# A graph network kernel: more groups of gathered rows fetched outside GpSimd's queue, from lists of byte offsets

## What is computed

```python
def reference(x, src, dst, edge_attr_32, ...):
    h = relu(layernorm(x))
    neigh1 = segment_sum(h[src], dst) * inv_deg          # round 0
    neigh2 = segment_sum(neigh1[src], dst) * inv_deg     # round 1
    x = x + 0.5 * neigh1 + 0.5 * neigh2
    h = relu(layernorm(x))
    for W_msg, W_edge, W_root, b in layers:              # rounds 2 and 3
        msg = h[src] @ W_msg + edge_attr_32 @ W_edge
        agg = segment_max(msg, dst)                      # 0 where a node has no edge
        h = leaky_relu(agg + h @ W_root + b)
    return x + h
```

## Time and profile before

| | |
|---|---|
| Time, median of 3 runs | 12477.9 us (12459.53 to 12489.42) |
| Span of the profiled execution, first to last instruction | 8075.9 us |
| The profiled execution's time around the span | not given on the page |
| POOL busy | 5983.3 us (74%), 6410 instructions |
| PE busy | 5063.4 us (63%) |
| DVE busy | 3315.1 us (41%) |
| ACT busy | 1517.2 us (19%) |
| Granted PE clock, mean share of full speed | 0.678 |
| DMAs of one row: SP, ACT, tail | 10240, 5120, 256 |
| Indirect DMAs of POOL | 6128 |

### The profile page before, as it was taken

The page is one execution under the profiler, slowest core; times in us unless marked ns, Lnnn a source line. Parts: engine busy times, 40 slices in busy tenths (PEclk is TensorE's granted clock), DMA queues, the critical chain, the costliest instruction groups (busy, mean ns, idle before and its releaser), DMA issues.

```text
span 8075.9 us, 156597 instructions
## 1 busy us (share of the span) xinstructions
PE 5063.4 (63%) x26211; PEld 3792.9 (47%) x26211; DVE 3315.1 (41%) x7073; ACT 1517.2 (19%) x5246; POOL 5983.3 (74%) x6410
## 2 busy tenths in 40 slices
PE   3444444445444444444677888787787788878878
PEld 2333333334333333333555655565575565556556
DVE  5444444445433333333533433333343343333335
ACT  2000000001000000000322333333342333333334
POOL 6777777776777777777677777777767777777776
PEclk7555555556555555555677888888797787888888
DMA  3111111111211111111144434444433443444443
GB/s 92 42 42 41 42 41 42 41 41 46 57 42 42 41 42 41 41 41 41 41 94 93 98 89 96 93 98 93 92 72 92 97 98 87 97 93 97 93 92 79
DMA packets 337350, 553.38 MB, mean 69 GB/s; under 512 B 212648, under 2 KB 212648, under 8 KB 311848
## 3 DMA queue, kind: packets, MB, share of 16 engines
q0 software_dynamic: 196096, 301.60, 18.2%
q1 hardware_dynamic: 129796, 243.57, 11.9%
q10 hardware_dynamic: 10788, 2.16, 0.2%
HBM read 521.97 MB, written 24.87 MB: 68 GB/s over the span
## 4 chain that ended last, share of the span: by engine, by line
POOL 53%; issue 21%; PE 11%; SPq 9%; DMA 3%; DVE 2%; ACT 1%; DVEq 0%; ACTq 0%; POOLq 0%
POOL rows L449 53%; SPq L296 5%; SPq L319 3%; PE ps L702 3%; PE ps L700 3%; DMA rows<-table,src_sb 2%; PE ps L724 2%; PE ps L807 1%; SPq L302 1%; PE ps L713 1%; DMA arena<-in_eat 1%; PE ps L681 0%; PE ps L818 0%; ACT arena L493 0%; DMA table<-arena 0%
## 5 line engine op out<-in xcount | busy, mean ns | idle before, releaser
L449 POOL DMA_INDIRECT rows<-table,src_sb x6128 | 5790.9, 945 | 1958.6 <-issue 1849.1
L681 PE MATMUL ps<-arena,rows 128*98 128x128 f32 (+1 forms) x6088 | 1513.6, 429 | 2097.1 <-DMA rows<-table,src_sb 1446.2
L681 PEld LDWEIGHTS ps<-arena,rows 128*98 128x98 f32 (+1 forms) x6088 | 1259.8, 276 | 2373.4 <-DVE comp L927 1990.2
L942 DVE TENSOR_TENSOR_SCAN arena<-arena,ps 96x512 f32<-96x512 f32 x782 | 997.6, 1276 | 2433.9 <-PE ps L702 2409.3
L927 DVE TENSOR_TENSOR comp<-comp,ps 98x128 f32 (+1 forms) x3128 | 894.7, 286 | 2158.4 <-PE ps L681 1841.9
L700 PE MATMUL ps<-arena,we 32*96 32x512 f32 x1564 | 993.7, 719 | 765.1 <-DMA rows<-table,src_sb 415.9
L702 PEld LDWEIGHTS ps<-ident,rows 128*96 128x96 f32 x6168 | 823.5, 187 | 714.4 <-issue 714.4
L910 DVE TENSOR_TENSOR arena<-ps,meta 128x512 f32<-128x512 f32 x1564 | 1050.7, 672 | 29.2 <-issue 25.7
L518 ACT COPY comp<-ps 96x128 f32 x3128 | 818.8, 262 | 1057.6 <-PE ps L724 796.4
L702 PE MATMUL ps<-ident,rows 128*96 128x128 f32 x6168 | 1013.5, 316 | 0.0
L724 PE MATMUL ps<-arena 128*96 128x128 f32 x6256 | 932.8, 299 | 0.9 <-ACT arena L509 0.9
(11 more groups left out here) (104 smaller groups left out, 1404.2 us busy)
## 6 DMA issues: line engine op xcount, KB each, us to landing
side<-table SPq DMA_DIRECT2D x10240, 0.4 KB
arena<-flags SPq DMA_DIRECT2D x194, 768.0 KB
rows<-table,src_sb POOLq DMA_INDIRECT x6128
side<-table ACTq DMA_DIRECT2D x5120, 0.4 KB
arena<-in_eat SPq DMA_DIRECT2D x194, 256.0 KB
table<-arena SPq DMA_DIRECT2D x56, 336.0 KB, 2.8
out<-xs SPq DMA_DIRECT2D x13, 336.0 KB
tail<-table SPq DMA_DIRECT2D x256, 0.4 KB
```

The source lines that it names most:

```text
L449: pool.indirect_dma_start(rows[:, g % RING, j, 0:D], None, tables[r][:, :], bass.IndirectOffsetOnAxis(src_sb[:, c:c + 1], 0)).then_inc(lan ...
L681: m = pe.matmul(ps[0:w, at + k * P:at + (k + 1) * P], got[k][:, 0:w], hot[:, j % HOTS, k, :], start=True, stop=True)
L942: dve.tensor_tensor_scan(run[:, slot % SCANS], fe[0:D, slot // UNIT, q * W:(q + 1) * W], ps[0:D, ROWS + slot % 2 * BANK:ROWS + slot % 2 * ...
```

## The change

`PLAN[r][e]` is now (first, step, n): n groups from `first` on, `step` apart; a group that would fall on place 0 or 1 of its sweep moves to place 2. In the sums these are groups 50, 94, 140, 186, 234, 278, 324, 370 on SP and 44, 90, 138, 182, 228, 274, 322, 366 on ACT, 16 in a round. In the maxima SP takes 60, 122, 186, 246, 308, 370, and ACT, which took none, 92, 182, 274, 362: 10 in a round.

A new input `order` holds `src` in edge order, one row of 512 numbers for each group. SP loads the rows of the groups aside, and that of the last group, into partitions of the new tile `low` (whose partition 0 is `base`), and DVE multiplies them by 384 once, so they are byte offsets (three more steps in `prep`). `side_rows` and `tail_rows` load 32 neighbouring numbers at once and use each as the offset of a DMA of 384 bytes, with no product between. SP and ACT in the sums, and SP in the maxima, issue a group as 16 such blocks; in the maxima SP spreads the blocks over the feature loads ahead of the group, and PE waits on one semaphore for each of the four batches.

In the maxima ACT's sweeps are unrolled, and each step of `extract` ends with `fetch_pair`: on even groups a load of 12 offsets and six DMAs, on odd groups the other six, 43 pairs for a group aside.

```diff
-PLAN = {r: {0: (9, 2), 1: (9, 3)} for r in (0, 1)} | {r: {0: (9, 0)} for r in (2, 3)}
+BLOCK = 32
+PAIR = 12
+PLAN = {r: {0: (48, 46, 8), 1: (44, 46, 8)} for r in (0, 1)} | {r: {0: (60, 62, 6), 1: (92, 90, 4)} for r in (2, 3)}
...
-SIDES = {r: {e: (SWEEPS - 1) // span for e, (span, _) in PLAN[r].items()} for r in PLAN}
-ASIDE = {r: {(b + 1) * PLAN[r][e][0] * RING + PLAN[r][e][1]: (e, b) for e in PLAN[r] for b in range(SIDES[r][e])} for r in PLAN}
+SIDES = {r: {e: [g + max(0, 2 - g % RING) for g in range(first, first + step * n, step)] for e, (first, step, n) in PLAN[r].items()} for r in PLAN}
+ASIDE = {r: {g: (e, b) for e in SIDES[r] for b, g in enumerate(SIDES[r][e])} for r in PLAN}
+LISTS = {(0, 0): 32, (1, 0): 32, (0, 1): 64, (1, 1): 64, (2, 0): 96, (3, 0): 96, (2, 1): 112, (3, 1): 112}
+ENDING = 32 + len(SIDES[0][0])
...
+        table_bytes = [t.rearrange("n d -> (n d)").bitcast(U8) for t in tables]
...
-        base = sb("base", [1, COLS], I32)
+        low = sb("low", [P, COLS], I32)
+        base = low[0:1, :]
...
-        def side_rows(engine, r, e, b, p):
-
-            span, seat = PLAN[r][e]
-            at = bass.ds(b * (span * RING * GRP) + (span * RING + seat) * GRP, GRP)
-            for k, row in enumerate(numbers(engine.engine, src_sb[p:p + 1, at], N - 1)):
-                engine.dma_start(side[p:p + 1, e, k, 0:D], tables[r][bass.ds(row, 1), :]).then_inc(side_in[r, e][k % 2], 16)
+        def side_rows(engine, r, e, b, h):
+
+            k, p0 = h * BLOCK // P, h * BLOCK % P
+            at = LISTS[r, e] + b
+            for p, byte in enumerate(numbers(engine.engine, low[at:at + 1, h * BLOCK:(h + 1) * BLOCK], (N - 1) * (4 * D)), p0):
+                engine.dma_start(side[p:p + 1, e, k, 0:D].bitcast(U8), row_of(r, byte)).then_inc(side_in[r, e][k], 16)
 
         def tail_rows(engine, r):
 
-            for p in range(REST):
-                row, = numbers(engine.engine, src_sb[p:p + 1, WHOLE:WHOLE + 1], N - 1)
-                engine.dma_start(tail[p:p + 1, 0, 0:D], tables[r][bass.ds(row, 1), :]).then_inc(tail_in, 16)
+            first = GRP * (GROUPS - 1)
+            for p0 in range(0, REST, BLOCK):
+                at = (WHOLE - first) * P + p0
+                for p, byte in enumerate(numbers(engine.engine, low[ENDING:ENDING + 1, at:at + BLOCK], (N - 1) * (4 * D)), p0):
+                    engine.dma_start(tail[p:p + 1, 0, 0:D].bitcast(U8), row_of(r, byte)).then_inc(tail_in, 16)
+
+        def row_of(r, byte):
+            return table_bytes[r][bass.ds(byte, 4 * D)].rearrange("(a n) -> a n", a=1)
 
         def side_sums(engine, r, e):
 
             for s in range(2):
                 engine.wait_ge(tstored[r][s], 16 * (CHUNKS // 2))
+            engine.wait_ge(prep, PREP_ALL)
             if e == 0:
-                engine.wait_ge(prep, PREP_ALL)
                 tail_rows(engine, r)
-            span, seat = PLAN[r][e]
-            with engine.Fori(0, SIDES[r][e]) as b:
-                engine.wait_ge(picked[r], b * (span * RING) + (seat + 1))
-                for p in range(P):
-                    side_rows(engine, r, e, b, p)
+            for b, g in enumerate(SIDES[r][e]):
+                if b:
+                    engine.wait_ge(picked[r], SIDES[r][e][b - 1] + 1)
+                for h in range(W // BLOCK):
+                    side_rows(engine, r, e, b, h)
...
+            for r, e in ((0, 0), (0, 1), (2, 0), (2, 1)):
+                for b, g in enumerate(SIDES[r][e]):
+                    at = LISTS[r, e] + b
+                    sp.dma_start(low[at:at + 1, 0:W], order[g:g + 1, :]).then_inc(s_lists, 16)
+            sp.dma_start(low[ENDING:ENDING + 1, 0:W], order[GROUPS - 1:GROUPS, :]).then_inc(s_lists, 16)
...
-                span, seat = PLAN[r][0]
-                units = 2 * span
-                with sp.Fori(0, SIDES[r][0]) as b:
-                    sp.wait_ge(rows_ps[r], b * (span * RING) + (seat + 1))
-                    for t in range(units):
-                        unit(b * span + (1 + t // 2), t % 2, UNIT)
-                        for p in range(t * P // units, (t + 1) * P // units):
-                            side_rows(sp, r, 0, b, p)
-                with sp.Fori(SIDES[r][0] * span + 1, SWEEPS - 1) as i:
+                t = 2
+                for b, g in enumerate(SIDES[r][0]):
+                    first = t
+                    if b:
+                        first = SIDES[r][0][b - 1] // UNIT + 1
+                        while t < first:
+                            unit(t // 2, t % 2, UNIT)
+                            t += 1
+                        sp.wait_ge(rows_ps[r], SIDES[r][0][b - 1] + 1)
+                    for t in range(first, g // UNIT):
+                        unit(t // 2, t % 2, UNIT)
+                        share = g // UNIT - first
+                        for h in range((t - first) * (W // BLOCK) // share, (t - first + 1) * (W // BLOCK) // share):
+                            side_rows(sp, r, 0, b, h)
+                    t = g // UNIT
+                if t % 2:
+                    unit(t // 2, 1, UNIT)
+                    t += 1
...
-                    if g >= RING:
-                        pool.wait_ge(used, (g - RING if g - RING not in ASIDE[r] else g - 2 * RING) + 1)
+                    before = g - RING
+                    while before in ASIDE[r]:
+                        before -= RING
+                    if before >= 0:
+                        pool.wait_ge(used, before + 1)
...
-                def extract(i, n, seen, here):
-
+                def extract(i, n):
+
+                    ahead = None
                     for j in range(n):
                         g = i * RING + j
                         own_part(i, j)
@@ -550,6 +564,29 @@
                             copy_running(g - 1, j - 1)
                         if after(g, 2):
                             windows(g - 2, j - 2)
+                        ahead = fetch_pair(g, ahead)
+
+                def fetch_pair(g, ahead):
+
+                    b = sum(at <= g - 2 for at in SIDES[r][1])
+                    if b == len(SIDES[r][1]):
+                        return None
+                    first = (SIDES[r][1][b - 1] + 3 if b else 2) // 2 * 2
+                    if g < first:
+                        return None
+                    at = (g - first) // 2 * PAIR
+                    if g == first and b:
+                        act.wait_ge(rows_ps[r], SIDES[r][1][b - 1] + 1)
+                    if at >= W:
+                        return None
+                    n = min(PAIR, W - at)
+                    of = LISTS[r, 1] + b
+                    if g % 2 == 0:
+                        ahead = numbers(act.engine, low[of:of + 1, at:at + n], (N - 1) * (4 * D))
+                    for q in range(g % 2 * PAIR // 2, min(n, (g % 2 + 1) * PAIR // 2)):
+                        k, p = (at + q) // P, (at + q) % P
+                        act.dma_start(side[p:p + 1, 1, k, 0:D].bitcast(U8), row_of(r, ahead[q])).then_inc(side_in[r, 1][k], 16)
+                    return ahead
...
-                    sweeps(act, r, extract)
+                    for i in range(SWEEPS):
+                        extract(i, RING if i < SWEEPS - 1 else LAST)
...
-                        for k in range(2):
-                            pe.wait_ge(side_in[r, e][k], (b + 1) * (P * GRP * 8))
+                        for k in range(GRP):
+                            pe.wait_ge(side_in[r, e][k], (b + 1 + (len(SIDES[2][e]) if r == 3 else 0)) * (P * 16))
...
+            dve.memset(low[LISTS[2, 0]:P, 0:W], 0).then_inc(xpad, 1)
...
+            dve.wait_ge(s_lists, 16 * (len(ASIDE[0]) + len(ASIDE[2]) + 1))
+            for at, n in ((LISTS[0, 0], len(SIDES[0][0]) + 1), (LISTS[0, 1], len(SIDES[0][1])), (LISTS[2, 0], P - LISTS[2, 0])):
+                step(dve.tensor_scalar(low[at:at + n, 0:W], low[at:at + n, 0:W], float(4 * D), None, ALU.mult))
...
+    order = np.pad(np.asarray(src), (0, fill)).reshape(GROUPS, W)
+    srcs = by_batch(order)
```

25 lines of the change are left out of this document (14 added, 11 removed).

## The result

The changed kernel takes **11633.45 us** (median of 4 runs, 11630.24 to 11651.21); before, in 4 runs beside them, 12471.42 (12459.53 to 12489.42). The ratio is 0.9328, 95% interval 0.9305 to 0.9351. The forecast was 12368 with a range of 12300 to 12520: the sign was right, the size wrong by 735 us. 838 us went where 110 were forecast.

What follows compares the result with a forecast made beforehand. POOL's chain of gathers, 1.249 us each, was taken as the bound: 88 fewer take 109.9 us off the span (8075.9 to 7966). With 4402.0 us outside it carried unchanged, 12477.9 - 109.9 = 12368 us, range 12300 to 12520.

Steps and rivals of the forecast that it cites:

- the sign: Whole kernel: faster, chance 0.73; same 0.07; slower 0.20.
- The step that failed: Time around the profiled span: the median's extra 4402.0 us, found in no row, were carried unchanged into the forecast.
- Rival 4: The 4402 us are POOL's gathers running slower outside the profile, 1.97 us each; 88 save 173, time 12305; chance 0.08.
- Rival 5: The 4402 us grow with the program, which has more unrolled instructions: slower by an unpriced amount; chance 0.03.
- 88 gathers x 1.249 = 109.9: POOL's chain: 22 more groups aside remove 88 gathers at 1.249 us each, 109.9 us off.
- The batch: SP's and ACT's 512 row DMAs in the sums: 207 and 205 us, both inside the interval of 219.8.
- The load of 32: Loading 32 offsets for the row DMAs: eight accesses of four, 2.2 us a load.
- rivals 2 and 3: Load of 32 dearer: 3.8 us, time 12548, chance 0.09; or a round trip per register: 7.2 us, 13880, 0.04.
- After the batch: Side rows in the sums: landing before PE uses them takes some 5 us, leaving 8 to 10 us of room.
- The start: First sum: SP's tail fetch 27 us; first side rows 18 us late on SP, 31 on ACT; cost 0, at most 5.
- The maxima: SP's batch 234 us in over 290; ACT's group with its new fetch 4.8 us against POOL's 4.995; nothing added.
- Rival 1: ACT bounds the maxima at 5.3 us a group: 150 us lost in all, net +40, time 12518; chance 0.14.

Runs made afterwards that it cites:

- e1: The kernel before, unchanged, run again with a profile where nothing steps: 8095.73 us, span 8094.0.
- f1: The changed kernel with no group aside, where the engines step: 9548.76 us, ratio to before 0.7594.
- e12: The changed kernel with no group aside, where nothing steps: 8220.91 us, ratio to before 1.0178.
- f3: The changed kernel with only 3 groups aside on SP and 3 on ACT per sum, 3 on SP per maximum, where engines step: 9718.95 us.
- e8: The changed kernel's new fetch with the old number of groups aside, where the engines step: 10404.33 us, against 12557.16 of before.
- e10: The changed kernel, unchanged, where nothing steps: 8010.22 us in one run, against 8075.76 of before.
- e2: The changed kernel's new fetch with the old number of groups aside, where nothing steps: 8068.48 us.
- e9: The changed kernel with ACT fetching nothing, SP's groups aside kept, where the engines step: 11748.06 us.
- e6: The changed kernel with offsets loaded four at a time instead of 32, where the engines step: 12352.14 us.
- g1: The changed kernel with all its groups aside and gathers of 64 partitions instead of 128, where the engines step: 11749.26 us.

## Why the prediction was wrong, point by point

**The step that failed** is the last one: "The median is 12477.9, 4402.0 us more than the profiled span, and no row shows what they are. I carry them unchanged." e1 and all later runs show 1.7 to 2.9 us outside the span. The 4402 us lie *inside* the span of the timed executions. Such a loss is 1328 us with no group aside at all (f1 against e12), and it grows with the batches that miss their interval (f3, e8, the changed kernel). It therefore depends above all on whether the fetchers' batches fit, which is what the change alters. Rival 4 had the place half right (the missing time goes with POOL's work) but priced it by gather, 1.97 us each. A gather costs 1.249 in both; it is the other engines that slow down. Rival 5, growth with the program, has the wrong sign: the changed kernel is the more unrolled one (though it executes 150312 instructions and not 156597) and is faster. The check named in the last sentence of the forecast, a time that moves by a very different amount, is what came true. That 4402 of 12478 us have no row was reason enough for a far wider range than 12300 to 12520: nothing in the trace vouched for the timed runs.

**The sign was luck.** The forecast had the time fall because 88 gathers leave POOL's chain. In the timed executions the 22 further groups aside *cost* over 1200 us (e8 against the changed kernel); what outweighed them is some 2100 us from the faster fetch, which the forecast counted as cover and gave no gain of its own.

**88 gathers x 1.249 = 109.9.** Right as a price. Where nothing steps 65.5 us came (e10, one run). Where they step the term has no meaning: the chain isn't POOL's.

**The batch.** SP 201, ACT 207 where nothing steps (forecast 207, 205). Where they step, 337 to 381 on SP in the sums, over the interval of 219.8 by more than half: the terms of the sum (225 ns, 29 ns) were still the medians, but the mean of a row is 0.7 us.

**The load of 32.** 2.05 to 2.12 us in e2, e10 and, as a median, in the changed kernel (2054 ns), forecast 2.2. The rivals' values, 3.8 and 7.2, fall, and with them rivals 2 and 3 in the forms given. The Trainium skill, page "Runtime: NRT & Kernel Launch", section "Instruction fetch mechanics", has about 200 ns per register "even for bulk"; the page speaks of loads from HBM. The trace, whose loads come from a tile in SBUF, differs for aligned neighbours: 2121 / 32 = 66 ns each.

**After the batch.** This is the mis-sized term where nothing steps: 5 us forecast, 15 + 4 measured. ACT's cycle is 226 us and not some 210, 6 over the interval. In the first sum the first batch is some 30 us late by its start and seven more cycles add 6 us each, of which the ring swallows 35. POOL's two sums take 36.5 and 20.0 us more than gathers x 1.249, where before had 7.0 and 0.5. These 49 us cover the 43 that the span misses (8008.5 against 7966); the 6 between are less than two executions of before differ by.

**The start.** SP's tail fetch takes 23.44 us and its side rows begin at 111.58 (forecast 27 and some 111); PE waits 26.0 us at most. As forecast, and inside the ring.

**The maxima.** Where nothing steps, POOL does its 1522 gathers in 1900.5 us, 0.5 *less* than 1522 x 1.249: SP's batches of 260 to 287 us (forecast 234) and ACT's six DMAs a group are free. Rival 1, ACT as the bound, falls there. ACT in e10, behind the first group aside of round 2, as in the earlier trace rows:

```profile
4449.49 0.47 ACT L522 COPY arena<-ps 128x384 f32<-128x384 f32 x1
4450.02 1.37 ACT L531 COPY comp<-ps 96x128 f32 x4
4452.21 2.12 ACTq L588 DMA_DIRECT2D side<-table  x6
4454.43 0.48 ACT L522 COPY arena<-ps 128x384 f32<-128x384 f32 x1 [3.04 <-PE ps L750]
```

4.94 us for this group, with a wait at its end, and 4.26 for the next (to 4458.69): near the forecast of 4.8 and under 4.995. Where they step, POOL's two maxima take 2430 and 2449 us, against 2297 to 2298 with nothing aside (f1), though there are 40 gathers fewer in each. There the fetch costs time, and it is SP's: its batches take 340 to 368 us, over their 62 groups (some 300 us at POOL's pace), and with ACT's fetch left out (e9, 16 gathers more in each) the maxima take 2491 and 2476 us, no less. PE hardly waits for the side rows themselves there (23.7 us) but for the edge features that SP issues between them: 174.1 us in the changed kernel, 425.6 in e9.

**What stays open.** No trace of the kernel *before* on a stepping chip exists: that its batches there are longer than its interval of 350 us is argued from e6 and e8, whose batches are 401 and 481 us with fewer instructions for a row, and from the 2100 us between before and e8. Not shown. Open as well are what makes instructions and semaphores late beside the gathers, whether the two are one thing, and how much of the loss in the sums is due to each.

## What to carry to other kernels

Here a run's time was never over 2.9 us more than its own span; where a profiled span and the median differ by more, the profile is not of the kind of execution that was timed. In such a case say what would follow if the difference lay inside the span, and run the kernel once more before costing anything by that trace. Work given to another queue needs slack for that queue's worst pace, not its usual one: here two fetchers with 6% of slack made the whole pipeline theirs once their rows took 0.7 us and not 0.4, and there the kernel with nothing aside was 24% faster than before, and 2% slower where nothing steps. Count the time from a batch's last issue to its use as a term of its own.

## What the runs showed of the hardware

- In some sets of runs, each on its own chip (medians of before 12471 to 12578 us; 8076 and 8077 in the others), sequencer instructions of SP, ACT and DVE come 0.7 us or a multiple apart while POOL issues indirect gathers: 51 row DMAs of SP in 58 us against 152 in 58 us with POOL waiting. No register instruction that starts over 8 us after the last gather takes 0.6 us. POOL's gathers are 945 to 947 ns in both kinds.
- Beside the gathers semaphores are late there as well: 2.2 us (median) from PE's last product to DVE's scan in f1, 0.04 in e12.
- The steps do not lessen with half the rows for each gather (g1: 372 us a batch, 11749 us in all), nor with one fetcher in place of two (e9: 11748).
- A gather of 64 rows is hardly cheaper than one of 128: 904 against 945 ns, 1.21 against 1.249 us from one to the next.
- A load of 32 aligned neighbouring registers takes 2.05 to 2.12 us, 64 to 66 ns each; for single ones the working of the prediction gives an estimate of 215 from the earlier trace rows.
- From the issue of ACT's last one-row DMA to PE's use of it, 13.7 to 15.4 us pass beside running gathers in 14 of 16 batches (e10).
